# Two transformer blocks on one core: a new order of all work, scan tiles that share banks, and another start and end

## The reference

```python
# block 0
mod = silu(condition) @ Wada + bada                    # shift, scale, gate for attention and MLP
xm = layernorm(x, g1, be1) * (1 + sc_a) + sh_a
x = x + gt_a * attention(xm)                            # 16 heads of 16, causal softmax
xm = layernorm(x, g2, be2) * (1 + sc_m) + sh_m
x = x + gt_m * (gelu(xm @ W1 + b1) @ W2 + b2)
# block 1
h = gamma(w) * layernorm(hidden) + beta(w)
q, k, v = split(h @ Wqkv.T + bqkv)
out = softmax(q @ k.T) / sqrt(256) @ v                  # no mask
h1 = out @ Wp.T + bp + hidden
return (gamma(w) * layernorm(h1) + beta(w)) + h1
```

## Time and profile before

| | us |
|---|---|
| three runs | 1238.06, 1238.27, 1231.66 |
| median | 1238.06 |
| the profiled execution | 1238.01 |
| its span, first to last instruction | 1236.3 |
| TensorE, matmuls in flight | 1165.5 (94%) |
| TensorE, weight loads | 592.4 (48%) |
| VectorE | 847.7 (69%) |
| ScalarE | 663.4 (54%) |
| GpSimd | 279.2 (23%) |
| DMA, mean of the span | 72 GB/s |

### The profile page before, as it was taken

How to read it: one execution, slowest core, us unless ns; L and a number is a source line. 1 busy time by engine, 2 the same in 40 slices (tenths; PEclk the granted TensorE clock), 3 DMA queues, 4 the chain that set the end, 5 groups by cost and what they waited for, 6 DMA issues and landing times.

```text
span 1236.3 us, 18439 instructions
## 1 busy us (share of the span) xinstructions
PE 1165.5 (94%) x6604; PEld 592.4 (48%) x6604; DVE 847.7 (69%) x1779; ACT 663.4 (54%) x1186; POOL 279.2 (23%) x378
## 2 busy tenths in 40 slices
PE   7888999999999999999999999999989999999995
PEld 5434654464454644555345644546445553445332
DVE  4835498637886579836887379855788368854775
ACT  1172245656557465565556465565655656454573
POOL 1133032311332024301233013320243002310003
PEclk9899999999999999999999999999999999999999
DMA  4603031302432032500523024410425005201211
GB/s 168 205 2 103 10 115 36 112 9 75 109 93 65 18 111 74 139 2 19 162 46 115 2 80 104 105 54 18 117 68 139 1 2 152 51 18 38 80 33 43
DMA packets 59189, 89.34 MB, mean 72 GB/s; under 512 B 12914, under 2 KB 23762, under 8 KB 59098
## 3 DMA queue, kind: packets, MB, share of 16 engines
q1 hardware_dynamic: 58078, 87.35, 25.3%
q10 hardware_dynamic: 1020, 0.81, 0.2%
HBM read 24.41 MB, written 4.70 MB: 24 GB/s over the span
## 4 chain that ended last, share of the span: by engine, by line
PE 61%; DVE 22%; SPq 5%; ACT 4%; DMA 3%; issue 3%; POOL 1%; ACTq 0%; DVEq 0%; POOLq 0%
PE X L1058 15%; DVE MX L776 12%; PE X L1109 9%; PE X L1085 9%; PE OP L959 9%; PE X L992 8%; PE SC L971 8%; SPq L430 4%; DVE STAT L785 2%; ACT E L637 2%; DMA OC<-OE 2%; DVE XN L825 2%; DVE XR L892 1%; DVE TMP L888 1%; PE X L1073 1%
## 5 line engine op out<-in xcount | busy, mean ns | idle before, releaser
L776 DVE TENSOR_REDUCE MX<-X 128x1 f32<-128x512 f32 (+3 forms) x1024 | 532.2, 582 | 180.0 <-PE X L995 96.5
L637 ACT ACTIVATE E<-SC 128x512 f32<-128x512 f32 (+1 forms) x864 | 446.0, 589 | 331.8 <-PE SC L971 266.8
L992 PE MATMUL X<-KS,QS 96*128 96x512 bf16 (+3 forms) x1024 | 298.3, 346 | 15.0 <-DVE MX L776 10.6
L971 PE MATMUL SC<-QS,KS 99*128 99x512 bf16 (+3 forms) x1024 | 265.6, 342 | 12.4 <-ACT E L637 6.5
L959 PE MATMUL OP<-E,V 128*32 128x512 f32 (+3 forms) x2048 | 209.4, 527 | 5.1 <-ACT OE L653 5.0
L992 PEld LDWEIGHTS X<-KS,QS 96*128 96x128 bf16 x1024 | 97.1, 98 | 172.0 <-DVE MX L776 61.1
L971 PEld LDWEIGHTS SC<-QS,KS 99*128 99x128 bf16 x1024 | 90.7, 97 | 147.3 <-ACT E L637 82.9
L555 POOL TENSOR_SCALAR_AFFINE_SELECT E<-E 128x512 f32<-128x512 f32 x128 | 87.1, 685 | 240.0 <-ACT E L637 240.0
L1109 PE MATMUL X<-XT,W 128*128 128x512 f32 x256 | 122.0, 610 | 1.2 <-ACT XT L668 1.2
L1085 PE MATMUL X<-XT,WQKV 128*128 128x512 f32 x256 | 118.3, 608 | 1.5 <-ACT XT L668 1.4
L1058 PE MATMUL X<-W,HID 128*128 128x256 f32 x512 | 115.3, 381 | 0.3 <-ACT HID L688 0.3
(11 more groups left out here) (92 smaller groups left out, 923.1 us busy)
## 6 DMA issues: line engine op xcount, KB each, us to landing
QS<-PART SPq DMA_DIRECT2D x192, 128.0 KB, 2.4
KS<-PART SPq DMA_DIRECT2D x192, 128.0 KB, 2.5
OC<-OE SPq DMA_DIRECT2D x56, 128.0 KB, 3.8
RB<-recip_sums SPq DMA_DIRECT2D x56, 128.0 KB, 2.6
XIN<-in_x SPq DMA_DIRECT2D x8, 512.0 KB, 4.9
ROW<-row_vectors SPq DMA_DIRECT2D x8, 512.0 KB, 3.5
out<-OUT SPq DMA_DIRECT2D x7, 512.0 KB, 3.2
W<-in_w SPq DMA_DIRECT2D x2, 1024.0 KB, 7.1
```

Source lines behind the costliest of these rows:

```text
L637: a.activation(E[:, at["tick"].index() % 3, heads, lo:T], SC[(at["head"].index() + j) % 3][:, 0:len(banks[j]) * (T - lo)] .rearrange("p (h ...
L776: v.reduce_max(MX[:, qt, h:h + 1], X[at["bank"].index() % BANKS][:, 0:w], AX.X, negate=True)\
L971: ins = t_.matmul(SC[(at["head"].index() + j) % 3][:, cols], KS[stacks(layer, b)][0:ALL_ROWS, 4 * g + h, kt * P:kt * P + P], QS[stacks(lay ...
L992: ins = t_.matmul(bank[:, 0:w], QS[stacks(layer, b)][0:CUT_ROWS, h, qt * P:qt * P + P], KS[stacks(layer, b)][0:CUT_ROWS, h, 0:w], start=Tr ...
```

## The change

The three lists are new from beginning to end. They hold the same chunks, the same numbers of `a`, `p`, `o` and `t`, and fewer `s` (233 to 180 in HEAD, 128 to 108 in RING, 151 to 144 in TAIL). `EARLY` is 6, now in new tiles. In layer 0, one tile of the first query tile holds four heads of 128 columns, one of the second two heads of 256; the other two query tiles stay alone. The causal matmul is one for a tile, its columns repeated for each head, and DVE's reduction gives one maximum for each head. Layer 1's tiles are the same.

At the start, DVE zeroes `WARM`, and PE multiplies it 14 times into `SC[2]` before it waits for anything else, and once after each of the first four modulation columns. x is loaded first on ACT's queue. `first_modulation` comes after DVE's norm. `q0` of b=0 starts when half of `XT` is there. POOL fills `V` ahead of the other constants. At the end, the last `proj1` starts on half of `OC`, two of the four statistics follow the first half of `TMP`, and `RH` is added in halves. (In the code the split of the statistics is in every `proj1`, that of `RH` in the last alone, and that of `OC` in the grouped `proj0` too.)

```diff
-EARLY = 9
+EARLY = 6
 HEAD = """
-    stat_a norm_a turn_a q0 stackq0 k0 stackk0 mods rows s v0 s s s s s s s s s s s s s s s s s s s s s s s s s
-    s s s s s s s nm0_0 s s max0_0 s s s s s s s s a s s s s row0 s p a s nm0_1 s keep0 p s s s a s max0_1 p o a
+    stat_a norm_a turn_a q0 k0 stackq0 mods stackk0 v0 rows s s s s s s s s s s s s s s s s s nm0_0 max0_0
+    s s s s s s s s s s nm0_1 s row0 a s s keep0 s p s a s max0_1 nm0_2 p s s s s a p a max0_2 o s s s p a
...
 RING = """
-    nm0b s s recip1 a max0b s s s p s a s p s s t s a s o s s p s a s scale1 s p o row1 a s t s p proj1 a s s p
-    o s a p a p s s s o s t a keep0 s p s s s a s gain1 p o close1 a nm1a stat_a max1a s v1 p norm_a a o t s
...
-    up_6 max1b s o s s up_7 t s s a s s down_0 s p down_1 s a s s p down_2 down_3 a o s p s s a s s p s s s s a
-    s norm_1 s o s p s s s a s s s s s p turn_1 a s nm0a s s t max0a s p q1 a s s o p s k1 s""".split()
+    row0 a s s s stackq1 p o a s p s s s s t o s s s s stackk1 a p a s s p s a s nm0b s o s s s s pack1
+    recip1 p a s s max0b p a p s s row1 s s s s s s t a p s s o s s a s s p o a scale1 s s p t s proj1 o a
+    p s s s a p s a p s s s gain1 o s t a p a nm1a s s s p a p keep0 close1 o stat_a max1a v1 o norm_a t
+    pack0 a p s turn_a a s s recip0 q0 p s s s a o p s s hold1 a s s p s s scale0 o a s s s stackq0 p proj0
+    a s s p k0 norm_m v0 turn_m s s a s s s p up_0 up_1 up_2 s t a s s s o s s s nm1b up_3 up_4 up_5 p
+    max1b up_6 up_7 o stackk0 s s s a s s down_0 down_1 down_2 s p s s t a down_3 p o a s s s p s a norm_1
+    s s s p o t a s s s p s turn_1 s a s s nm0a s s p s s a s s p o max0a a q1 p k1""".split()
...
+def scan_tiles(layer):
+    if layer == 1:
+        return [(slice(h, h + 1), qt) for h in range(H) for qt in range(TT)]
+    return [(slice(h, h + n), qt) for g in range(0, H, 4) for qt, n in enumerate((4, 2, 1, 1)) for h in range(g, g + 4, n)]
...
@@ DVE scan
-                v.reduce_max(MX[:, qt, h:h + 1], X[at["bank"].index() % BANKS][:, 0:w], AX.X, negate=True)\
+                psum = X[at["bank"].index() % BANKS][:, 0:(heads.stop - heads.start) * w]
+                v.reduce_max(MX[:, qt, heads], psum.rearrange("p (h k) -> p h k", k=w), AX.X, negate=True)\
@@ PE scan
-                ins = t_.matmul(bank[:, 0:w], QS[stacks(layer, b)][0:CUT_ROWS, h, qt * P:qt * P + P],
-                                KS[stacks(layer, b)][0:CUT_ROWS, h, 0:w], start=True, stop=layer == 1)
+                n = heads.stop - heads.start
+                for h in range(n):
+                    ins = t_.matmul(bank[:, h * w:h * w + w], QS[stacks(layer, b)][0:CUT_ROWS, heads.start + h, qt * P:qt * P + P],
+                                    KS[stacks(layer, b)][0:CUT_ROWS, heads.start + h, 0:w], start=h == 0, stop=layer == 1)
                 if layer == 0:
-                    ins = t_.matmul(bank[:, qt * P:w], ID16[:], CAUSAL[:], start=False, stop=True)
+                    ins = t_.matmul(bank[:, 0:n * w].rearrange("p (h k) -> p h k", k=w)[:, :, qt * P:w], ID16[:],
+                                    CAUSAL[:].unsqueeze(1).to_broadcast([P, n, P]), start=False, stop=True)
@@ PE, the start
+            def warm(times):
+                for _ in range(times):
+                    t_.matmul(SC[2][:], WARM[:, 0:P], WARM, start=True, stop=True)
+            pe.wait_ge(warm_dve, 1)
+            warm(BEFORE_FIRST)
+            pe.wait_ge(ada_load, 16)
             pe.wait_ge(set_dve, SILU_READY)
-            pe.wait_ge(ada_load, 16)
             for n in range(4):
                 ins = modulated(n, SC[0])
+                warm(1)
@@ SP and ACT
-            sp.dma_start(XIN[:], x[0].rearrange("(t p) d -> p t d", p=P)).then_inc(x_dma, 16)
+            act.dma_start(XIN[:], x[0].rearrange("(t p) d -> p t d", p=P)).then_inc(x_dma, 16)
             act.dma_start(VF[:], vecs).then_inc(vec_load, 16)
@@ DVE
-                    if what == "norm_a" and b == 0:
-                        first_modulation()
...
+                    if what == "norm_a" and b == 0:
+                        first_modulation()
@@ DVE proj1
-                    wait(dve, dense_dve, at["by_dve"].at(1, 2))
-                    stats(at, TMP)
+                        wait(dve, dense_dve, at["by_dve"].at(1, tp + 1))
+                        if tp == 0:
+                            token_stats(TMP, (0, 1))
+                    stats(at, TMP, (2, 3))
@@ PE proj
-                        wait(pe, dense_act, at["by_act"].at())
+                        wait(pe, dense_act, at["by_act"].at(1, -1))
+                        second = at["by_act"].at()
+BEFORE_FIRST = 14
```

More of the change, by code:

```diff
@@ new lines @@
+    s s s s s s s s s s nm0_1 s row0 a s s keep0 s p s a s max0_1 nm0_2 p s s s s a p a max0_2 o s s s p a
+    o t s p s s a p s nm0_3 a p a o p a o t p a stat_a p max0_3 a p o a p norm_a turn_a o t a fold0_0
+    fold0_1 p a p a p a o p o fold0_2 t fold0_3 merge0 q0 proj0 k0 norm_m v0 turn_m up_0 up_1 up_2 stackq0
+    stackk0 s s s up_3 s up_4 s s up_5 s s s s up_6 s s s s up_7 s s s s s s s down_0 s nm0a down_1 max0a
+    down_2 s s s down_3 a s s s s p norm_1 a s p a s s p s a o turn_1 s s s s row0 keep0 q1 s stackq1 k1 p
@@ new lines @@
+    a o s p a t stackk1 s p a s s s p s nm0b stat_a a p v1 s s o norm_a max0b s s s o t turn_a s s s s q0 s
+    s a p s s s a p s s s a p a s s s p o s s a s s s p o s t a s s p s s a p s a p s o s nm1a s o s s t
+    pack0 max1a s s recip0 s s v0 s s a s s p s s a p s s s s a s o scale0 s p s s a proj0 norm_m p stackq0
+    o a t k0 turn_m p s s s s a s s p up_0 up_1 up_2 up_3 up_4 s s stackk0 a s s s s o p s s nm1b a s max1b
+    p up_5 up_6 up_7 a hold1 s s s o p down_0 down_1 down_2 a s s p down_3 t a o p s a s p s s norm_1 a s s
@@ L256, in one_list @@
         elif what == "s":
-            layer, b, h, qt = tiles.pop(0)
-            if h % (H // 2) == 0 and qt == 0:
+            layer, b, heads, qt = tiles.pop(0)
+            if heads.start % (H // 2) == 0 and qt == 0:
                 at["halves"].n += 1
-            work(at, "scan", (layer, h, qt), b)
+            work(at, "scan", (layer, heads, qt), b)
             at["scan"].n += 1
@@ L793, in work @@
                 if kind == "scan":
-                    layer, h, qt = what
-                    scan(at, layer, b, h, qt)
+                    layer, heads, qt = what
+                    scan(at, layer, b, heads, qt)
                     return
@@ L1051, in bank, with by_token @@
                     return X[marks["down"]]
-                def by_token(k, rows, weights, tiles, depth):
+                def by_token(k, rows, weights, tiles, depth, second=0):
                     psum = bank(k)
@@ L1079, in work @@
                         pe.wait_ge(qkv_load[n], 16)
-                    wait(pe, dense_act, marks["xt"])
+                    first = what == "q0" and b == 0
+                    wait(pe, dense_act, marks["half_xt" if first else "xt"])
                     for t in range(2):
@@ L1083, in work @@
                         for kt in range(KT):
+                            if first and t == 0 and kt == 1:
+                                wait(pe, dense_act, marks["xt"])
                             lo = (2 * side + t) * P
```

99 lines of the change are left out of this document (52 added, 47 removed).

## The result

The changed kernel takes 1227.36 us (median, 1224.05 to 1234.15) where the kernel before takes 1237.53 in the same rounds: ratio 0.9923, 95% interval 0.9906 to 0.994. So it is 10.2 us faster, where I forecast 24.8, and the 1227 lies 14 us above the forecast 1213. Its profiled execution took 1228.83 us with a span of 1227.1. The time lies inside the range, at the place of rival (a).

A forecast was written before the change was run, and what follows sets the result against it. PE was taken as the first bound, with DVE limiting the prologue. Start 9.6, first row 0.5, seven rows 14 and end 0.7 summed to 24.8 us: 1238.0 to 1213, range 1199 to 1230.

The forecast's parts named there:

- rival (a): Whole kernel: rows keep their length, only start and end gain, 1227 us; chance 0.19.
- Part 4: Seven rows from b=1 on: fewer waits 1.7, DVE slack 0.7, new waits minus 0.4; 2.0 us each, 14 in all.
- the wait for NMP: Steady rows, PE before the transposes of the maxima: most of its 1.9 us wait goes, taken as 1.7 per row.
- the 141 to 142 that the prediction named: Sign to look for in the profile after: steady rows of 141 to 142 us.
- I cost these at nothing: Steady rows, SP and POOL queues that steps move past: no cost; without cover, 1 to 2 us a row each.
- a rival for the clock at the start alone: Start: clock falls back after idle matmuls, or these delay first tiny ones; start gains 4 to 5, 1218 us; chance 0.06.
- Part 2: The start, up to the first score matmul: 9.6 us earlier, near 47; bounds 4 and 11.
- its DMA lands long before, 1.5 us more: Start, max0_0 now behind tile 17: its transfer lands early and PE runs ahead of DVE, 1.5 us gained.
- Part 1: Shared scan tiles: 160 fewer reductions at 69 ns each where DVE bounds, 150 where waited for; 0.5 us on PE.
- rival d: Scan: merged tiles reach DVE late, 3.1 us lost per batch row, 1252 us; chance 0.05.
- Parts 3 and 5: First row to 116.7: 0.5 us from moving q0 and early proj; the end: 0.7 us from split steps, less later attention.

The follow-up runs named there:

- the run with the wait and the doubled scans: Changed kernel with GpSimd waiting for the normalisation before cutting k0, eight scans around row1 made twice, second layer's weights loaded later: 1207.79 us, ratio 0.9766.
- the run with the wait: Changed kernel, lists untouched, with GpSimd waiting for the normalisation before it cuts k0 (every batch row but b=2's): 1211.45 us, ratio 0.981.

## Why the prediction was wrong in size

**Part 4 is the step that failed.** It forecast 2.0 us for each of seven rows, 14 in all. From the first mark to the last, the seven took 982.5 us instead of 980.7: 1.8 longer. The gain that it counted was there: the wait for NMP went as said, and once two costs are taken away the steady rows last 142.0 us on average (the run with the wait and the doubled scans, 710.2 for five) against 144.3 before, 2.2 less per row, at the edge of the 141 to 142 that the prediction named. What failed is its last sentence, "I cost these at nothing", on the queues that steps are moved past. I followed `hold1` and the stacks, and not `k0`, whose cut on GpSimd is 3.2 us of work that the list put beside `norm_m`. That is worth 15.9 us by the medians of the run with the wait and 14 by the ratios, which is about the whole miss of 14.4 us. A row that priced it, the two means of L892, was in the trace of before. I had looked for new waits; this cost is no wait but a longer duration, and my sum took every duration from the kernel before. The same sentence passed over `recip1`, which the new list puts right behind `pack1`: in four of five steady passes VectorE waits 0.45 to 1.65 us there.

**The clock in the rows is missing from the sum.** The earlier trace rows shows full speed in both rows, and I carried that over. (One steady row of before, from 235.9 to 382.5, did hold a fall of 3.4 us and lasted 146.6.) The new list has a run of eight scans with nothing else for TensorE. The passes in which the clock fell are 2.6 to 4.3 us longer than the one in which it didn't, and with redundant work in place of the falls the median is 2.6 us lower, although that work takes time itself. The rows and the executions at different clocks show that falls cost time. How much of the 10.8 us is theirs, the medians only make likely. My forecast had a rival for the clock at the start alone.

**Part 2** forecast 9.6 us up to the first score matmul, and it was 7.6. The steps up to the reductions are right within 0.5 us (`q0` at 11.41 for 11.8, 7.11 for 7.1, reductions at 33.79 for 33.3). The term that was mis-sized is the last: "its DMA lands long before, 1.5 us more". It landed 6.11 us after its issue, beside the loads of the weights, and TensorE idled 1.44 for it. That gain didn't come, and even when it does (the run with the weights later) little of it reaches the end. On the way to the reductions two terms missed in opposite senses: the idle matmuls took 4.85 us and not 6, and the granted clock fell to half for 6.8 us from 21.7 on, so that `v0` took 5.23 us and not 3.5.

**Part 1.** Busy time fell by 15.8 us for 160 reductions, 99 ns each, between my 69 and 150. The fixed time that the Trainium skill gives (VectorE: DVE Perf Modes, section "The TRN2 errata") made it 20 us, so this trace lies between the page and the row. The size was fine. The way to the time was not as told: nothing measurable in the old order, and in the new one something up to 27 us, which no run bounds from below. The merged tile as a new wait (rival d) did not come: VectorE's idle time behind TensorE fell from 180.0 to 170.3 us.

**Parts 3 and 5.** The first mark is 7.7 us ahead, so the first row gave 0.1 where I said 0.5. The last mark to the end is 3.3 us shorter (140.6 against 143.9), and the row before it 5.2 (129.9 against 135.1). I had 0.7 and 2.0. Neither difference can be put down to the edits as it stands. Tiles moved across the marks: VectorE has 197 instructions between the last two marks before and 167 after, of which the merge explains 20, and 8 more than before in the tail. And the tail of before had a fall of the clock in it:

```profile
1092.40:1236.30 143.90, 127.99 (x612) 55.54 (x610) 80.35 (x154) 70.92 (x132) 17.65 (x27) 0.95 0.15 42
...
1092.70:1233.70 141.00, 124.62 (x612) 55.02 (x611) 80.64 (x154) 71.05 (x132) 17.48 (x27) 0.97 0.15 43
```

The second line is the run with the new start alone, which has the old end and still needs only 141.0 us. So most of the 3.3 us is the clock. What the trace does show of part 5 is the stretch from the start of the last addition into `TMP` to the end: 7.9 us (from 1219.21) against 8.9 (from 1227.36), where I had 0.7 for the statistics. The 5.2 us of the row before come with the new list: the two runs with the old order have 135.1 (tiles alone) and 134.8 (start alone) there. Which of its moves gave them stays open.

**Rival (a)** gave 1227, the measured time, by "the rows keep their length". They did not. The steady rows became 2.2 us longer each, 10.8 in all, and the last two stretches gave 8.5 back. The number is right and its reason isn't, which only the marks could show: two misses of opposite sign in one sum.

## What to carry to other kernels

When an order is rewritten, list for each elementwise step on VectorE what GpSimd does at the same time, before and after. A mean that differs between two groups of the same operation and shape (here 1113 against 692 ns) is the price of such a neighbour, and it moves with the order. In this kernel a run of work in which TensorE waited for VectorE at every tile went with half the clock behind it, so look at the granted clock of each repeated pass and not at a mean, and look at what a run covers before breaking it up.

## What the runs showed of the hardware

- Four normalisations of 128x256 on VectorE took 1.37 us alone and 3.99 beside GpSimd's cut of 128x1024, one of them 2.29. GpSimd was hardly slowed (1.14 and 2.13 us, against 1.04 and 2.12).
- Of twelve executions of one kernel on one core, the extremes: 1224.05 to 1224.83 us at a mean granted clock of 0.986, 1233.05 and 1234.15 at 0.975 and 0.976.
- Adding 8 matmuls to every steady row did not cost time: the median is 2.6 us lower (the intervals overlap), and the granted clock stayed up in that place in all five passes.
- A reduction of 512 columns into 4 maxima lasted 682 ns and into 2 679, as long as into one (680).
- A transfer of 12 KB took 6.11 us with the DMA engines busy for 0.88 of the stretch from 33.8 to 49.0, and 2.36 us in the kernel before, with 0.09 from 54.22 to 56.58.
